# The slot table of a routed expert layer: loaded whole, by partition, and indexed on VectorE

## The reference, cut to what matters

```
xf = layernorm(x).reshape(4096, 512)
gate_scores = xf @ gate_W + gate_b                 # 4 experts
topk_scores, topk_idx = top_k(gate_scores, 2)
weights = softmax(topk_scores)
expert e:  h = relu(layernorm(xf @ W1[e] + b1[e]) * g1[e] + be1[e])
           layernorm(h @ W2[e] + b2[e]) * g2[e] + be2[e]
out = sum over the two chosen experts of weights * expert(xf)   (+ xf, + x)
```

## Time and profile before

| | |
|---|---|
| median of three runs | 1353.3 us |
| the profiled execution | 1347.39 us, its span 1345.5 us |
| TensorE busy | 1196.3 us (89%) |
| VectorE busy | 944.7 us (70%) |
| ScalarE busy | 739.7 us (55%) |
| GpSimd busy | 437.2 us (32%) |
| chain that ended last | TensorE 63%, issue 10%, SyncE's queue 8%, DMA 6%, VectorE 5% |
| granted TensorE clock, mean | 0.943 |

### The profile page before, as it was taken

One profiled execution on the slowest core, in us unless ns is written; L12 is line 12 of the kernel. 1 busy time (PEld: TensorE's weight loads), 2 busy tenths in 40 slices (PEclk: granted clock), 3 DMA queues, 4 the chain that ended last, 5 costly groups with the idle time before them and its releaser, 6 DMA issues.

```text
span 1345.5 us, 24589 instructions
## 1 busy us (share of the span) xinstructions
PE 1196.3 (89%) x6041; PEld 999.0 (74%) x6042; DVE 944.7 (70%) x2197; ACT 739.7 (55%) x2119; POOL 437.2 (32%) x392
## 2 busy tenths in 40 slices
PE   5698999999679999999999848979909999999993
PEld 4487888888568888888887737767708888888882
DVE  6687888887545777787888826667707777777773
ACT  4332333333257767757767613656607777777772
POOL 1000000000023314544543433346504555544542
PEclk9799999999769999999999968999959999999996
DMA  9545443444410112132112237883504444444443
GB/s 299 165 157 187 141 156 137 132 140 152 156 50 1 55 48 87 46 90 93 40 56 91 67 99 207 283 219 66 93 1 78 79 78 78 82 83 83 79 64 38
DMA packets 78802, 143.22 MB, mean 106 GB/s; under 512 B 22810, under 2 KB 27086, under 8 KB 76917
## 3 DMA queue, kind: packets, MB, share of 16 engines
q1 hardware_dynamic: 61541, 106.24, 24.5%
q0 software_dynamic: 17056, 35.21, 14.7%
q10 hardware_dynamic: 144, 1.05, 0.2%
HBM read 78.83 MB, written 67.83 MB: 109 GB/s over the span
## 4 chain that ended last, share of the span: by engine, by line
PE 63%; issue 10%; SPq 8%; DMA 6%; DVE 5%; POOL 3%; ACT 3%; POOLq 1%; DVEq 0%; ACTq 0%
PE banks L999 17%; PE banks L638 16%; PE banks L701 6%; PE banks L831 6%; PE banks L821 4%; PE banks L790 3%; PE banks L807 3%; SPq L585 2%; SPq L586 2%; DMA out<-rows,scatter_rows 2%; PE banks L847 2%; PE banks L1025 1%; ACT rows L1185 1%; DMA expert_parts<-operands 1%; PE banks L1011 1%
## 5 line engine op out<-in xcount | busy, mean ns | idle before, releaser
L999 PE MATMUL banks<-operands 128*128 x1608 | 394.7, 401 | 18.6 <-issue 6.2
L999 PEld LDWEIGHTS banks<-operands 128*128 128x128 f32 x1608 | 302.1, 191 | 90.3 <-issue 23.1
L638 PE MATMUL banks<-operands 128*128 128x512 f32 (+2 forms) x1224 | 299.8, 403 | 15.3 <-DVE operands L1405 9.3
L638 PEld LDWEIGHTS banks<-operands 128*128 128x128 f32 (+1 forms) x1224 | 232.4, 198 | 64.3 <-DVE operands L1405 8.4
L1082 ACT ACTIVATE operands<-banks 128x512 fp32r<-128x512 f32 (+3 forms) x328 | 192.1, 607 | 133.0 <-PE banks L807 46.4
L1405 DVE TENSOR_TENSOR operands<-banks,operands 128x512 fp32r<-128x512 f32 (+3 forms) x328 | 218.0, 682 | 64.2 <-ACT operands L1082 63.4
L1185 ACT ACTIVATE rows<-banks,score_shift 128x77 f32<-128x77 f32 x512 | 162.1, 369 | 30.2 <-DVE score_shift L1613 27.4
L1082 ACT ACTIVATE operands<-rows 128x512 fp32r<-128x512 f32 (+2 forms) x73 | 54.5, 751 | 176.2 <-DVE rows L1484 135.2
L1331 ACT ACTIVATE banks<-banks,param_cols 128x128 f32<-128x128 f32 x268 | 99.2, 430 | 82.3 <-PE banks L1025 82.3
L2020 DVE BATCH_NORM_STATS2 moe_stats<-banks 128x6 f32<-128x512 f32 x134 | 93.0, 694 | 66.4 <-issue 45.3
L1185 ACT ACTIVATION_READ_ACCUMULATOR rows<-banks,score_shift 128x1 f32 x512 | 127.1, 251 | 0.0
(11 more groups left out here) (175 smaller groups left out, 1675.5 us busy)
## 6 DMA issues: line engine op xcount, KB each, us to landing
expert_parts<-operands SPq DMA_DIRECT2D x32, 512.0 KB, 3.3
operands<-expert_parts SPq DMA_DIRECT2D x8, 2048.0 KB, 9.2
rows<-in_x SPq DMA_DIRECT2D x8, 1024.0 KB, 5.5
rows<-in_L_ffn_W SPq DMA_DIRECT2D x32, 256.0 KB, 3.7
x_rows<-rows SPq DMA_DIRECT2D x8, 1024.0 KB, 4.4
rows<-x_rows SPq DMA_DIRECT2D x8, 1024.0 KB, 5.7
xf_rows<-rows SPq DMA_DIRECT2D x32, 256.0 KB, 2.7
out<-rows SPq DMA_DIRECT2D x32, 256.0 KB, 2.5
```

The source lines that it names most:

```text
L638: last = nc.tensor.matmul(dst, stationary(a, k), moving(b, k), start=(t == 0 and k == 0), stop=(t == len(terms) - 1 and k == n_k - 1))
L999: last = nc.tensor.matmul(dst, stationary[:, a, k, :], weights[:, bass.ds(e, 1), w, a2, k, :].rearrange("p e f -> p (e f)"), start=False, ...
```

## The change

A table row s is now stored at partition s mod 128, column s div 128: `slots` gets three more steps that turn the row number into (s mod 128) * 152 + s div 128, so NROUTE is 30. The whole table then has 152 columns of 8 bytes for each partition, 1216 bytes in one piece, and a tile of 128 slots is one column. SyncE loads the whole table twice, into two buffers: once when four chunks are scattered, and once when all are. `plan_row` holds the column number, so `plan_bases` loses its factors of 128. VectorE's `gather_rows` loads the tile's column into a register, copies both words of the column to `tile_slots` and the token numbers to the index tile. It does so for all tiles: for tiles 0 and 1, 2 and 3 in `last_turn`, for tile 4 ahead of the tiles, and for the others in `c_tile` where the index copy was. GpSimd makes no copies of its own. In `last_turn` GpSimd waits for the first load ahead of the scatters of chunk 4, and VectorE ahead of the first fetch. The parts of `plan_early` move: part 0 from ahead of `pT_lo_part(c, 2, (0, 1))` to behind `q_lo(c + 1, 2)` of turn 6, part 1 behind `slots`, part 2 to the start of `last_turn`. Chunks 5 and 7 use buffer 1 of `slot_ix`, chunk 6 buffer 0. In `tiles_of` only VectorE waits for the second load.

```diff
-ROUTE_CHOSEN, ROUTE_COUNTED, ROUTE_SHIFTED, ROUTE_WEIGHED, NROUTE = 6, 10, 12, 20, 27
+ROUTE_CHOSEN, ROUTE_COUNTED, ROUTE_SHIFTED, ROUTE_WEIGHED, NROUTE = 6, 10, 12, 20, 30
...
+        tables = [f_at(kb, 2 * TABW).bitcast(I32).rearrange("p (n w) -> p n w", w=2) for kb in (58, 24.75)]
...
-        def tiles_of(engine, tile):
+        def tiles_of(engine, tile, late=None):
...
             engine.wait_ge(plan_ready, 2)
-            engine.wait_ge(slots_in, 16 * NSLOT)
+            if late is not None:
+                engine.wait_ge(*late)
...
-            def load_slots(i):
-
-                row = sp.value_load(plan_row[0:1, bass.ds(i, 1)], min_val=0, max_val=NE * REG - P)
-                sp.dma_start(tile_slots[:, bass.ds(i, 1), :].rearrange("p i w -> p (i w)"),
-                             slots_d[bass.ds(row, P), :]).then_inc(slots_in, 16)
+            def load_table(n):
+                sp.dma_start(tables[n], slots_d.rearrange("(p n) w -> p n w", p=P)).then_inc(slots_in, 16)
...
-            sp.wait_ge(plan_ready, 1)
             sp.wait_ge(scattered, 16 * 2 * TPC * EARLY_CH)
-            with sp.Fori(0, EARLY) as i:
-                load_slots(i)
+            for i in range(2):
+                sp.wait_ge(base_out[i], 16 * 2 * (last - 1))
+            load_table(0)
...
-            sp.wait_ge(plan_ready, 2)
-            sp.wait_ge(scattered, 16 * 2 * (NT - TPC))
-            sp.wait_ge(scattered_aside, 16 * 2 * TPC)
-            with sp.Fori(EARLY, NSLOT) as i:
-                load_slots(i)
+            sp.wait_ge(scattered, 16 * 2 * TPC * (NCH - 2))
+            sp.wait_ge(scattered_aside, 16 * 2 * TPC * 2)
+            load_table(1)
...
             def weighed_be2(n, u, e):
 
+                act.wait_ge(gix_ready, 2 * n + u + 1)
...
                 step(V.tensor_copy(slot_ix[aside][:, :, :], kval[:, 1, :, :]))
+                step(V.tensor_scalar(slot_low[:, :, :], slot_ix[aside][:, :, :], P - 1, None, ALU.bitwise_and))
+                step(V.tensor_scalar(slot_col[:, :, :], slot_ix[aside][:, :, :], P.bit_length() - 1, None,
+                                     ALU.arith_shift_right))
+                step(V.scalar_tensor_tensor(slot_ix[aside][:, :, :], slot_low[:, :, :], float(TABW),
+                                            slot_col[:, :, :], ALU.mult, ALU.add))
...
-            def gather_rows(n, u):
-
-                need(dve, gathered[u], 16 * n)
-                V.tensor_copy(gix[u][:, :], tile_slots[:, bass.ds(2 * n + u, 1), 0]).then_inc(gix_ready, 1)
+            def gather_rows(i, u, table):
+
+                column = dve.value_load(plan_row[0:1, bass.ds(i, 1)], min_val=0, max_val=TABW - 1)
+                need(dve, gathered[u], 16 * (i // 2))
+                V.tensor_copy(tile_slots[:, bass.ds(i, 1), :], table[:, bass.ds(column, 1), :])
+                V.tensor_copy(gix[u][:, :], table[:, bass.ds(column, 1), 0]).then_inc(gix_ready, 1)
...
                 if after >= 5:
-                    gather_rows(n + 2 + u, 1 - u)
+                    gather_rows(i + 5, 1 - u, tables[early >= FRONT])
...
             def last_turn(c):
                 normalise(c, 0)
-                scatter(c - 3, 0)
-                scatter(c - 3, 1)
                 normalise(c, 1)
                 ln3_pow(c - 1, 0)
-                scatter(c - 3, 2)
-                scatter(c - 3, 3)
+                pool.wait_ge(slots_in, 16)
+                scatter(c - 3, 0)
+                scatter(c - 3, 1)
                 normalise(c, 2)
                 for u in range(2):
-                    gather(0, u, own=True)
+                    gather(0, u)
                 normalise(c, 3)
                 ln3_pow(c - 1, 1)
+                scatter(c - 3, 2)
+                scatter(c - 3, 3)
...
-                if own:
-                    need_alone(pool, slots_in, 16 * EARLY, pool_passed)
-                    G.tensor_copy(gix[u][:, :], tile_slots[:, bass.ds(i, 1), 0]).then_inc(first_gix, 1)
-                    need_alone(pool, first_gix, i + 1, pool_passed)
-                else:
-                    need_alone(pool, gix_ready, i + 1 - 5, pool_passed)
+                need_alone(pool, gix_ready, i + 1, pool_passed)
...
-            gather(1, 0, own=True)
-            for j in range(TPC):
-                scatter(last - 2, j)
+            gather(1, 0)
+            for j in range(2):
+                scatter(last - 2, j, aside=1)
             ln3_pow(last, 0)
-            gather(1, 1, own=True)
+            for j in range(2, TPC):
+                scatter(last - 2, j, aside=1)
+            gather(1, 1)
             ln3_pow(last, 1)
```

More of the change, by code:

```diff
@@ L1754, in slots @@
                 step(V.tensor_reduce(kval[:, 1], kth[:, :, :, :], AX.X, ALU.add))
-                if not aside:
-                    need(dve, scattered, 16 * 2 * TPC * min(c, NCH - 2) if isinstance(c, int) else 16 * 2 * TPC * c)
+                if aside:
+                    need(dve, scattered_aside, 16 * TPC * (c - (NCH - 3)))
+                else:
+                    need(dve, scattered, 16 * 2 * TPC * (NCH - 3 if isinstance(c, int) and c == NCH - 2 else c))
                 step(V.tensor_copy(payload[aside][:, :, :, 0], tok[:, :].unsqueeze(2).to_broadcast([P, TPC, 2])))
@@ L1789, in plan_bases @@
                 number, rows = tile_no[:, 0:count], tile_row[:, 0:count]
-                plan_step(V.tensor_scalar(jump[:, :], tiles[:, :], -float(P), float(REG), ALU.mult, ALU.add))
-                plan_step(V.tensor_scalar(rows, number, float(P), None, ALU.mult))
-                if skipped is not None:
-                    plan_step(V.scalar_tensor_tensor(jump[:, 0:NE - 1], skipped[:, 1:NE], float(P), jump[:, 0:NE - 1],
-                                                     ALU.mult, ALU.add))
-                    plan_step(V.scalar_tensor_tensor(jump[:, 0:NE - 1], skipped[:, 0:NE - 1], -float(P),
-                                                     jump[:, 0:NE - 1], ALU.mult, ALU.add))
-                    plan_step(V.tensor_scalar(total[:, 0:1], skipped[:, 0:1], float(P), None, ALU.mult))
-                    plan_step(V.tensor_scalar(rows, rows, total[:, 0:1], None, ALU.add))
+                plan_step(V.tensor_scalar(jump[:, :], tiles[:, :], -1.0, float(REG // P), ALU.mult, ALU.add))
+                if skipped is None:
+                    plan_step(V.tensor_copy(rows, number))
+                else:
+                    plan_step(V.tensor_tensor(jump[:, 0:NE - 1], jump[:, 0:NE - 1], skipped[:, 1:NE], ALU.add))
+                    plan_step(V.tensor_tensor(jump[:, 0:NE - 1], jump[:, 0:NE - 1], skipped[:, 0:NE - 1], ALU.subtract))
+                    plan_step(V.tensor_scalar(rows, number, skipped[:, 0:1], None, ALU.add))
             def plan_rows(count):
@@ L1916, in b_turn @@
                     xf_features(c - 1, c, 3)
+                if planned:
+                    plan_early(0)
                 if back2:
@@ L1925, in b_turn @@
                     slots(c - 2, c)
+                if planned:
+                    plan_early(1)
                 q_lo(c + 1, 3)
@@ L1955, in last_turn @@
                 pT_lo_part(c, 1, (2,))
+                dve.wait_ge(slots_in, 16)
+                for u in range(2):
+                    gather_rows(u, u, tables[0])
                 x2_rows(c - 1, c, 2)
@@ L1980, in last_turn @@
                 xf_features(c - 1, c, 3)
+                for u in range(2):
+                    gather_rows(2 + u, u, tables[0])
                 gate_bias(c)
@@ L2121, in _ @@
             read_positions(tail)
-            slots(last - 1, tail, aside=1)
+            slots(last - 1, tail)
             for j in range(2, TPC):
@@ L2238, in last_turn, with gather @@
                 normalise(c, 0)
+                normalise(c, 1)
+                ln3_pow(c - 1, 0)
+                pool.wait_ge(slots_in, 16)
                 scatter(c - 3, 0)
                 scatter(c - 3, 1)
-                normalise(c, 1)
-                ln3_pow(c - 1, 0)
+                normalise(c, 2)
+                for u in range(2):
+                    gather(0, u)
+                normalise(c, 3)
+                ln3_pow(c - 1, 1)
                 scatter(c - 3, 2)
                 scatter(c - 3, 3)
-                normalise(c, 2)
-                for u in range(2):
-                    gather(0, u, own=True)
-                normalise(c, 3)
-                ln3_pow(c - 1, 1)
-            def gather(n, u, own=False):
+            def gather(n, u):
                 i = 2 * n + u
@@ L2299, in c_tile @@
                 if early == 0:
-                    gather(2, 0, own=True)
+                    gather(2, 0)
                 if early >= 2:
@@ L2305, in c_tile @@
                 if 1 <= early < 5:
-                    scatter(last - 1, 2 + (early - 1) // 2, aside=1, ks=((early - 1) % 2,))
+                    scatter(last - 1, 2 + (early - 1) // 2, ks=((early - 1) % 2,))
                 if 5 <= early < 13:
```

(14 more changed lines are left out.)

26 lines of the change are left out of this document (10 added, 16 removed).

## The result

The changed kernel takes 1298.91 us (median of 4 runs, 1297.48 to 1300.31) against 1353.36 (4 runs, 1351.11 to 1354.72): ratio 0.9599, 95% interval 0.9581 to 0.9618. Forecast were 1319 and a range of 1302 to 1335. The profiled execution took 1297.48 us, its span 1295.8, at a mean granted clock of 0.959 (0.943 before).

What follows compares the result with a forecast made beforehand. VectorE was taken to set the steady tiles' pace, with two slot-list loops causing pauses. Terms -34.9 - 18.3 - 3 + 2.5 + 4.5 + 13.2 + 2 = -34.0 from 1347.4, plus 5.9 offset, gave 1319.3 us; range 1302 to 1335.

Steps and rivals of the forecast that it cites:

- The late loop, -34.9: Tiles 17 to 24: one hidden 152 KB transfer replaces 38 loads, removing the pause and slow restart, -34.9 us.
- The early loop, -18.3 and -3: Turn 7: the early table load removes TensorE's pause, -18.3 us, and the cold stretch behind it, -3 us.
- Moves and added steps, 0 and +2.5: Plan parts moved in turns 6 and 7: zero, +-2; three slot steps per chunk: +2.5 us.
- fetches ahead of the loop, +4.5: Five register loads with two copies each on VectorE, four inside turn 7: +4.5 us, between 0 and 5.5.
- The fetch in the steady tiles, +13.2: Tiles 18 to 61: VectorE's fetch between addition and shift adds 0.3 us in each of 44 tiles, +13.2 us.
- that 0.63: Steady tiles: VectorE's wait for GpSimd's reciprocal root, 0.63 us each, taken as the only cover for added VectorE work.
- Rival A: Steady tiles: the fetches are hidden, pair 13.0 us, +13.2 and +2 go, 1303 us; chance 0.20.
- Rival B: Steady tiles: fetches cost double, 0.62 us instead of 0.3, pair 14.2, +14 us, 1333 us; chance 0.20.
- Rival D: Tiles: the register load waits until VectorE drains, so fetch and root run in sequence, 1.1 us a tile, 1372; chance 0.04.
- The front tiles, +2: Tiles 0 to 17: fetches with a constant index cost about 0.15 us each, the last six having room, +2 us.
- the competition of expert weights and gathers: 18 front tiles: a new wait where earlier-starting expert-weight loads compete with gathers would make the prediction wrong; no size given.
- The offset, 5.9 kept: Whole run: the median's 5.9 us above the profiled execution is kept, taking 1313.4 to 1319.3 us.

Runs made afterwards that it cites:

- 24 tiles written out: The kernel before with FRONT = 24 instead of 18, giving the late loop six tiles more: 1315.16 us against 1349.36, ratio 0.9752.
- 44 single loads: The changed kernel with its second whole-table load replaced by a SyncE loop of 44 single-column loads: 1338.50 us, ratio 0.9915.
- second profile: The kernel before, unchanged, profiled again: 1350.19 us, tile -1 at 831.69 (828.17 the first time).
- five-list run: The kernel before with the five lists needed first loaded alone, the other 24 behind xf's first stores: 1341.72 us against 1349.36, ratio 0.9938.
- added load: The changed kernel with a second, unused register load ahead of each fetch in the tiles: 1333.76 us, ratio 0.9853, pair of steady tiles 14.76.
- the test: The changed kernel with expert-weight loads from the third on held on SyncE until tile 0's epsilon addition: 1300.29 us, ratio 0.9633.
- combined version: The changed kernel with its whole table for tiles 0 to 28, 24 tiles written out, 38 single-column loads for the others: 1287.77 us, ratio 0.9520.

## Why the prediction was right or wrong

**The late loop, -34.9: right.** The stretch is 33.8 us shorter with the fetches of seven tiles in it, 1.1 us at the measured 0.155, which gives -34.9. 24 tiles written out took 35.1 out of it, and the 44 single loads brought the pause back.

**The early loop, -18.3 and -3: right in sum, with a mechanism left out.** The pause and the cold stretch are gone, and tile 0 came 16.3 us earlier (20.3 against the second profile) for a forecast 14.3. The prediction took the wait as the whole effect. In the five-list run the wait was gone and tile 0 moved by 8.3: the queue time behind it, of which the text said only that store and load order "gets earlier", holds about half, and would have been late next. That the sum came out is partly luck, since its small terms were never told apart:

**Moves and added steps, 0 and +2.5; fetches ahead of the loop, +4.5: not told apart.** They are below the 4 us by which two profiles differ at tile 0.

**The fetch in the steady tiles, +13.2: the step that failed.** The local step was right: the shift was forecast at 1.31 us behind the addition and stands at 1.30 (the first copy came 0.13 later than forecast, the rest closer behind it). What failed is the sentence "What is added to it there counts in full unless it fits in that 0.63". In the two tiles of a pair the shift comes 0.28 and 0.21 us later behind its addition (1.02 and 1.09 before), 0.49 in all and not 0.6, since the forecast's 0.3 was read in the tile with 1.02 alone. And the pair is only 0.31 longer: 0.18 is given back between the shift and the next addition, 0.11 of it ahead of the first long instruction behind the shift, and 0.07 in the loop's own register load, as in the kernel without the fetch's load. So a term was mis-sized: the mechanism, that what is added between addition and shift lengthens the tile, holds, but not in full. Against the kernel before the cost is 0.155 x 44 = 6.8 us where the sum has 13.2. Rival A (nothing, 13.0), the forecast (13.6) and the measured 13.3 lie evenly spaced: neither was nearer. Rival B (14.2) is not borne out in the steady loop: the added load shows 0.306 us, as in the earlier trace rows. An uncovered load costs its queue 0.62 us from start to start and 0.72 a tile: the row is the load alone, and its register arithmetic and hand-overs come on top. The Trainium skill (DMA: Bandwidth & Descriptors, Latency and other measured facts) gives a floor of about 600 ns for a `tensor_load`: the trace does not agree for the load itself, with 306 ns, and comes near it with the 620 ns from start to start. Rival D (no overlap of load and addition) is excluded by the pair of 13.31.

**The front tiles, +2: wrong in sign.** The prediction named the competition of expert weights and gathers as a danger, since the loads "start earlier than now". Starting earlier they also end earlier against the tiles, which is a gain: -3.3 in all, of which the test took back 2.

**The offset, 5.9 kept: wrong.** It came from one profile against a median, and it was spread. Against its own median of 1298.91 the changed kernel's profile is 1.4 low; the second profile of before is 2.6 low. A difference of one execution and a median is no term of a sum; it belongs in the range.

The steady tiles' 5.5, the front tiles' 5.3, the 4.9 of the other three stretches and the offset's 4.5 make the 20 us. Each is small, and all point the same way; the last two are in large part the spread of single profiles, and only the first two are terms with a cause that a run shows, the second of them in part.

## What to carry to other kernels

A loop of small indexed loads cost twice here: the consumer's wait, and everything that stands behind it in the queue; count both before you remove it, and try first whether a longer head start hides it. A register load was free when it was issued behind a 0.69 us instruction of its engine, and cost 0.7 us where nothing covered it: put it a step ahead of its use, not next to it. Where an engine waits for another in each tile, short instructions in front of that wait were free, and the same ones elsewhere were not.

## What the runs showed of the hardware that was not expected

A register load of 0.306 us in the trace costs 0.72 us of its engine's pace if nothing covers it, 0.19 where a wait of 0.6 covers most of it, and nothing behind a 0.69 us statistics instruction (pairs of 14.76, 13.31 and 12.94 against 12.93 without a load). A semaphore wait against a register's number on VectorE, for something long done, cost (13.27 - 13.02) / 2 = 0.13 us a tile. Loads of a kilobyte took SyncE 1.45 us each in the kernel before, 128 rows that follow each other in HBM, and 59.42 / 38 = 1.56 in the combined version, one column of the new layout, where the whole table of 152 KB takes one issue of 0.36.

Some small operations of VectorE took ten times as long as their neighbours: the cast of the earlier trace rows in the plan, and this one of 16 values a partition, which the kernel before has as well as the changed one:

```profile
764.42 2.10 DVE L1735 TENSOR_TENSOR gate_exp<-gate_exp,gate_sel 128x16 f32<-128x16 f32 x1
```

```profile
767.25 2.10 DVE L1732 TENSOR_TENSOR gate_exp<-gate_exp,gate_sel 128x16 f32<-128x16 f32 x1
```

```profile
767.07 2.26 POOL L2211 TENSOR_TENSOR rows<-rows,score_rec 128x1232 f32<-128x1232 f32 x1 [4.76 <-DVE score_rec L1618]
```

The second fence is the changed kernel's, and the third GpSimd's timeline beside it. Moving the plan freed the plan of its two such operations (725.45 and 740.61 before), but a comparison of the gate then took 1.86 us at 740.88. In each of these five cases GpSimd was at an operation on 1232 values, which began ahead of the small one, and the small one ended within 0.1 us of it. That the one holds the other up was not tested.
